# Attention scores from row-tiled products of q and k in place of stacked copies, and three heads of four transposed by DMA

## The reference: what is computed

```python
h = jnp.maximum(_layernorm(x, axis=-1), 0.0)
q = split_heads(h @ Wq.T); k = split_heads(h @ Wk.T); v = split_heads(h @ Wv.T)
bias = (adj + adj)[:, None]
a = jnp.einsum('bhnd,bhmd->bhnm', q, k) * D ** (-0.5) + bias
row_nonzero = jnp.any(a != 0, axis=-1, keepdims=True)
a = jnp.where(row_nonzero, a, -jnp.inf)
p = jax.nn.softmax(a, axis=-1)
p = jnp.where(jnp.isnan(p), 0.0, p)
o = jnp.einsum('bhnm,bhmd->bhnd', p, v)
x = x + merge_heads(o) @ Wo.T
```

## Time and profile before

| what | value |
|---|---|
| median of 3 runs | 1202.02 us (1201.95 to 1202.43) |
| the profiled execution, its own time | 1201.87 us |
| its span in the profile | 1200.1 us |
| PE (matmul) busy | 1131.5 us, 94% |
| PEld (weight load) busy | 803.0 us, 67% |
| DVE busy | 973.2 us, 81% |
| ACT busy | 973.3 us, 81% |
| POOL busy | 693.8 us, 58% |
| DMA queue q1 | 156.57 MB, 58.6% of 16 engines |

### The profile page before, as it was taken

One profiled execution on the slowest core, in us unless ns is written; L12 is line 12 of the kernel. 1 busy time (PEld: TensorE's weight loads), 2 busy tenths in 40 slices (PEclk: granted clock), 3 DMA queues, 4 the chain that ended last, 5 costly groups with the idle time before them and its releaser, 6 DMA issues.

```text
span 1200.1 us, 32321 instructions
## 1 busy us (share of the span) xinstructions
PE 1131.5 (94%) x10068; PEld 803.0 (67%) x10068; DVE 973.2 (81%) x3418; ACT 973.3 (81%) x3155; POOL 693.8 (58%) x939
## 2 busy tenths in 40 slices
PE   6789999999999999999999999999999999999997
PEld 5557766667766666766666776666776666776664
DVE  6888788888788888778888778888878887878884
ACT  3588888888888888888888888888888888888886
POOL 1346666656666656666655666655666655666655
PEclk9999999999999999999999999999999999999999
DMA  6345656565665665665565665655665565666654
GB/s 221 81 103 116 142 139 133 127 143 113 142 137 138 124 145 111 142 139 137 124 147 109 141 141 134 134 140 110 138 142 134 135 137 113 136 145 133 138 107 115
DMA packets 327193, 158.62 MB, mean 132 GB/s; under 512 B 279152, under 2 KB 287600, under 8 KB 327024
## 3 DMA queue, kind: packets, MB, share of 16 engines
q1 hardware_dynamic: 327024, 156.57, 58.6%
HBM read 47.45 MB, written 16.78 MB: 54 GB/s over the span
## 4 chain that ended last, share of the span: by engine, by line
PE 77%; DVE 17%; issue 4%; ACT 1%; DMA 1%; DVEq 0%; POOLq 0%; SPq 0%; POOL 0%; ACTq 0%
PE ps L998 44%; DVE k_stack L777 9%; PE ps L1014 9%; PE ps L1029 8%; DVE logits L727 6%; PE ps L1063 6%; PE ps L1068 5%; PE ps L878 2%; PE ps L1042 2%; DVE w_max L650 1%; ACT probs L527 1%; DMA w_nat<-in_L_gnn_Wq 1%; DVE x_res L804 0%; DVE row_min L727 0%; DVE w_lo L690 0%
## 5 line engine op out<-in xcount | busy, mean ns | idle before, releaser
L527 ACT ACTIVATE probs<-logits,row_min 128x256 f32<-128x256 f32 x1024 | 509.0, 502 | 67.1 <-DVE row_min L727 66.9
L727 DVE CUSTOM_DVE_ANT_0 logits<-ps,adj_s,sigma 128x256 f32<-128x256 f32 x1024 | 451.9, 479 | 52.5 <-PE ps L1014 50.4
L424 POOL TENSOR_TENSOR p<-probs,p 128x512 f16<-128x512 f32 x256 | 302.7, 1183 | 159.3 <-ACT p L540 158.6
L998 PE MATMUL ps<-ht_hi,w_hi 128*128 128x256 f16 x1024 | 280.4, 274 | 0.6 <-DVE q_lo L763 0.6
L998 PE MATMUL ps<-ht_hi,w_lo 128*128 128x256 f16 x1024 | 280.0, 273 | 0.0
L998 PE MATMUL ps<-ht_lo,w_hi 128*128 128x256 f16 x1024 | 279.8, 273 | 0.0
L1014 PE MATMUL ps<-k_stack,q_stack 96*128 96x256 f16 x1024 | 198.0, 275 | 38.7 <-DVE k_stack L777 38.7
L433 POOL TENSOR_TENSOR norm<-recip,some 128x256 f32<-128x256 f32 x128 | 85.7, 670 | 197.4 <-DVE some L744 197.3
L527 ACT ACTIVATION_READ_ACCUMULATOR probs<-logits,row_min 128x1 f32 x1024 | 198.5, 194 | 0.0
L1014 PEld LDWEIGHTS ps<-k_stack,q_stack 96*128 96x128 f16 x1024 | 82.8, 98 | 144.4 <-issue 63.0
L1029 PE MATMUL ps<-ident,probs 128*128 128x128 f32 x1024 | 154.1, 273 | 6.4 <-ACT probs_t L551 6.4
(11 more groups left out here) (86 smaller groups left out, 2065.9 us busy)
## 6 DMA issues: line engine op xcount, KB each, us to landing
xs<-in_x SPq DMA_DIRECT2D x34, 512.0 KB, 4.1
q_stack<-q_hi SPq DMA_DIRECT2D x256, 64.0 KB, 2.0
x_res<-in_x SPq DMA_DIRECT2D x32, 512.0 KB, 4.0
out<-x_res SPq DMA_DIRECT2D x64, 256.0 KB, 2.5
adj_raw<-in_adj SPq DMA_DIRECT2D x33, 256.0 KB, 4.8
q_stack<-q_lo SPq DMA_DIRECT2D x128, 64.0 KB, 2.0
pt<-p SPq DMA_TRANSPOSE x256, 3.1
w_nat<-in_L_gnn_Wq SPq DMA_DIRECT2D x1, 1024.0 KB, 6.0
```

Of the source, the lines that this page charges most:

```text
L424: g.tensor_tensor(p16[:, c % 2, k, 1], probs[:, h % 4].rearrange("p u n -> p (u n)"), p16[:, c % 2, k, 0], ALU.subtract).then_inc(p_split, 1)
L527: e = a.activation(probs[:, h % 4, u, :], logits[:, h % 4, u, :], ACT.Exp, bias=row_min[:, t.par(d), u, h:h + 1], scale=-1.0, accum_out=ro ...
L727: v.tensor_tensor_reduce(out=logits[:, h % 4, u, :], in0=ps[:, S_BANK + S_OF[h], N * u:N * u + N], in1=adj_s[:, t.par(d), u, :], scale=sig ...
L998: m = mm(o, l, r, start=start, stop=stop)
```

## The change

1. The stacks are gone. `scores` takes a whole group at once: for each half of the queries and each of the three products, the four heads in turn, each from the 32 partitions where its q and k lie. The four lie in four row tiles (32*128) of the array and write to four PSUM banks. It runs once every four steps, after the projection of steps 0, 4, 8 and 12, and waits until all eight logit units of the group before are done. q_hi, q_lo, k_hi and k_lo are doubled, by batch parity. The twelve DMAs to q_stack and the twelve copies to k_stack fall away.
2. `XJ = (0, 1, 2)`: three heads of four go by ScalarE rounding, GpSimd split and DMA transpose; only head 3 is transposed by TensorE. It goes to `AUX_BANK`, at the start of steps 0, 4, 8 and 12, and VectorE instead of ScalarE copies it out (`take_probs_t`). The bank of the transposed probabilities is freed. `AUX_USES` writes down the order in which the bank is used.
3. v is split when it leaves PSUM: ScalarE writes v_hi, and an fp32 copy of the columns of head 3 (v_y); VectorE writes v_lo (`take_v`) and frees the bank. GpSimd's `split_v` falls away.
4. Steps move: `values` comes ahead of the projection of its step, logits of a group come as 3, 3 and 2 units in the three steps after its scores, `turn_h` is at steps 5 and 9, layernorm at 3, adj_s at 7, the input of the residual at 4, the output DMAs at 12 and 14. Statistics, layernorm and loads of batches past the last one are left out. The maximum of Wo is found in the first slot instead of the second.

The core of the diff:

```diff
-XJ = (0, 2)
+XJ = (0, 1, 2)
 YJ = tuple(j for j in range(HC) if j not in XJ)
 NX, NY = len(XJ), len(YJ)
-S_OF = (0, 1, 2) * 5 + (1,)
...
+        q_hi = sb("q_hi", [P, 2, NC, N], F16)
+        q_lo = sb("q_lo", [P, 2, NC, N], F16)
+        k_hi = sb("k_hi", [P, 2, NC, N], F16)
...
-        q_stack = sb("q_stack", [NK * HD, 2, HC, NC, N], F16)
-        k_stack = sb("k_stack", [NK * HD, 2, HC, NC, N], F16)
-        v_sb = sb("v_sb", [P, 2, NU, D])
+        v_hi = sb("v_hi", [P, 2, NU, D], F16)
+        v_lo = sb("v_lo", [P, 2, NU, D], F16)
+        v_y = sb("v_y", [P, 2, NU, NC, NY, HD])
...
+        AUX_USES = [("h", 0, 0), ("h", 0, 1)]
+        for b in range(-1, NB + 1):
+            slot_uses = [(0, y_key(b, -1)), (4, ("y", b, 0)), (8, ("y", b, 1)), (12, ("y", b, 2)),
+                         (13, ("row", b + 1))]
+            slot_uses += [(9, ("h", b + 2, 0)), (12, ("h", b + 2, 1))] if b < 0 else \
+                         [(5, ("h", b + 2, 0)), (9, ("h", b + 2, 1))]
+            for at, key in sorted(slot_uses):
+                if 0 <= key[1] < NB and not (key[0] == "y" and NY == 0):
+                    AUX_USES.append(key)
...
-                    if s in (5, 6) and t.nxt:
-                        if s == 5:
-                            need(sp, scores_ready, H * t.batch(0))
-                        sp.wait_ge(pj_hi, 4 * t.batch(1) + 2)
-                        for j in range(HC):
-                            stack(t, q_stack, s - 5, q_hi, j, q_stacked)
-                    if s == 7 and t.nxt:
-                        for g in range(2):
-                            sp.wait_ge(pj_taken[g], pj_taken_at(t, g))
-                        for j in range(HC):
-                            stack(t, q_stack, 2, q_lo, j, q_stacked)
-                    if s in (14, 15) and t.prev:
...
-                        scale_adj(t)
+                    split_probs(t, s)
                     if s == 0 and t.prev:
                         spread_norm(t, -1, NC - 1)
                     if s % 4 == 0 and s >= 4 and t.cur:
                         spread_norm(t, 0, s // 4 - 1)
-                    split_probs(t, s)
-                    if s == 1 and t.cur:
-                        split_v(t)
-                    if s == 2 and t.nxt:
+                    if s == 3 and later(t, 2):
                         layernorm(t, 2)
+                    if s == 7 and t.nxt:
+                        scale_adj(t)
...
-                need(act, *turned_before(t, d, h))
+                b, c, j = t.batch(d), h // HC, h % HC
+                if j in XJ:
+                    need(act, p_split, NC * NX * b + by_dma(h) - NX + 1)
+                elif b + c > 0:
+                    act.wait_ge(aux_full, aux_after(*y_key(b, c - 1)))
...
-                a.activation(v_sb[:, t.par(d), u, :], ps[:, PJ_BANK + u, :], ACT.Copy, scale=DOWN)\
-                 .then_inc(pj_taken[u], 1)
+                a.activation(v_hi[:, t.par(d), u, :], ps[:, PJ_BANK + u, :], ACT.Copy, scale=DOWN)\
+                 .then_inc(v_hi_ready, 1)
+                for k, j in enumerate(YJ):
+                    a.activation(v_y[:, t.par(d), u, :, k, :],
+                                 ps[:, PJ_BANK + u, :].rearrange("p (c j d) -> p c j d", c=NC, j=HC)[:, :, j, :],
+                                 ACT.Copy, scale=DOWN).then_inc(v_hi_ready, 1)
...
-            def logit_rows(t, s):
-                d, h = head(t, s)
+            def logit_rows(t, c, first_unit, last_unit):
...
                     return
-                dve.wait_ge(scores_ready, H * t.batch(d) + (h + 1))
-                if h == 0:
-                    dve.wait_ge(adj_scaled, t.batch(d) + 1)
-                need(dve, probs_ready, H * t.batch(d) + (h - 3))
-                for u in range(NU):
-                    v.tensor_tensor_reduce(out=logits[:, h % 4, u, :], in0=ps[:, S_BANK + S_OF[h], N * u:N * u + N],
+                b = t.batch(d)
+                if first_unit == 0:
+                    dve.wait_ge(scores_ready, NC * b + (c + 1))
+                    if c == 0:
+                        dve.wait_ge(adj_scaled, b + 1)
+                for n in range(first_unit, last_unit):
+                    h, u = HC * c + n // NU, n % NU
+                    need(dve, probs_ready, H * b + (h - 3))
+                    v.tensor_tensor_reduce(out=logits[:, h % 4, u, :],
+                                           in0=ps[:, S_BANK + h % HC, N * u:N * u + N],
                                            in1=adj_s[:, t.par(d), u, :], scale=sigma[:, 0:1], scalar=3e38,
...
+            def take_v(t, d, u):
+                dve.wait_ge(v_hi_ready, (1 + NY) * (NU * t.batch(d) + u + 1))
+                v.scalar_tensor_tensor(out=v_lo[:, t.par(d), u, :], in0=ps[:, PJ_BANK + u, :], scalar=DOWN,
+                                       in1=v_hi[:, t.par(d), u, :], op0=ALU.mult, op1=ALU.subtract)\
+                 .then_inc(pj_taken[u], 1)
             def take_qk(t, j):
...
+            LOGITS = {1: (0, 3), 2: (3, 6), 3: (6, 8)}
             def slot(t):
                 for s in range(H):
-                    if t.prev and s in residual_steps(t):
-                        residual(t, residual_steps(t).index(s))
-                    logit_rows(t, s + 3)
...
+                    if t.prev and s in (10, 12):
+                        residual(t, (s - 10) // 2)
+                    if s == 1 and t.cur:
+                        take_v(t, 0, 1)
+                    if s == 15 and t.nxt:
+                        take_v(t, 1, 0)
+                    if s in (3, 5, 7, 9) and t.nxt:
+                        take_qk(t, (s - 3) // 2)
+                    if s % 4:
+                        logit_rows(t, (s + 3) // 4, *LOGITS[s % 4])
                     if s % 4 == 3 and t.cur:
                         invert(t, 0, s // 4)
...
-                            ln_statistics(t, 2, 1)
+                            for u in range(NU):
+                                ln_statistics(t, 2, u)
+                        if s == (5 if t.first else 2):
                             ln_mean_var(t, 2)
-                        if s in (3, 5, 7, 9):
-                            take_qk(t, (s - 3) // 2)
-                        if s in (9, 10, 11):
-                            stack_k(t, *((0, (0, 2)), (0, (1,)), (1, (0, 2)))[s - 9])
-                        if s in (11, 12, 13, 14):
-                            stack_k(t, *((1, (1,)), (2, (0, 2)), (2, (1,)), (3, (0, 2)))[s - 11])
-                        if s == 14:
-                            stack_k(t, 3, (1,))
-                        if s == (10 if t.first else 6):
-                            check_adj(t)
...
-                d, h = head(t, s)
+            def scores(t, c):
+                d, c = group(t, c)
...
+                if c == 0:
+                    for g in range(2):
+                        pe.wait_ge(pj_taken[g], (NJ // 2) * b + 2)
+                need(pe, logits_ready, NU * (H * b + HC * c))
+                Q, K = (q_hi, q_lo), (k_hi, k_lo)
                 for u in range(NU):
-                    m = mm(ps[:, S_BANK + S_OF[h], N * u:N * u + N], q_stack[:, t.par(d), j, c, P * u:P * u + P],
-                           k_stack[:, t.par(d), j, c, :], start=True, stop=True)
+                    for i, (x, y) in enumerate(THREE):
+                        for j in range(HC):
+                            m = mm(ps[:, S_BANK + j, N * u:N * u + N],
+                                   Q[x][HD * j:HD * j + HD, t.par(d), c, P * u:P * u + P],
+                                   K[y][HD * j:HD * j + HD, t.par(d), c, :], start=(i == 0), stop=(i == 2))
                 m.then_inc(scores_ready, 1)
...
                         o = ps[HD * j:HD * j + HD, PV_BANK, 0:N]
+                        h = HC * c + j
...
+                            m = mm(o, v_y[:, t.par(d), mh, c, YJ.index(j), :],
                                    probs_t[:, c % 2, YJ.index(j), mh, :], start=(mh == 0), stop=(mh == NU - 1))
                             continue
                         k = XJ.index(j)
                         for i, (a, b) in enumerate(THREE):
-                            m = mm(o, v16[:, t.par(d), a, k, mh, c, :],
+                            m = mm(o, (v_hi, v_lo)[a][:, t.par(d), mh, HD * h:HD * h + HD],
...
-                    if not t.first:
-                        scores(t, s + 4)
-                    elif s == H - 2:
-                        scores(t, H)
-                        scores(t, H + 1)
-                    elif s == H - 1:
-                        scores(t, H + 2)
-                        scores(t, H + 3)
+                    if NY and s == 0 and t.prev:
+                        turn_probs(t, -1, NC - 1)
+                    if NY and s % 4 == 0 and s >= 4 and t.cur:
+                        turn_probs(t, 0, s // 4 - 1)
+                    if s == 3 and t.prev:
+                        values(t, -1, NC - 1)
+                    if t.cur and s >= 4 and s % 4 == 3:
```

(14 more changed lines are left out.)

256 lines of the change are left out of this document (99 added, 157 removed).

## The result

The changed kernel takes 1217.92 us (median of 4 runs, 1217.49 to 1218.6); the kernel before took 1202.22 beside it. The ratio is 1.0125, interval 1.0106 to 1.0143: 1.3% slower, where 6.5% faster was forecast. The span grew from 1200.1 to 1215.7 us.

A forecast was written before the change was run, and what follows sets the result against it. TensorE was taken as the bound, its slot falling from 35.93 to 33.6 us: 31 slots give 72.2, plus 3.7 and 2.2 at the ends, 78.1 us off the 1200.1 span; predicted 1124 us, range 1085 to 1178.

The forecast's parts named there:

- whether the others cover: VectorE, ScalarE, GpSimd and DMA per slot: stay off the path; four steps of 2.1 us cover a 3.1 us DMA transpose.
- what would make the prediction wrong: Per group or slot: S above 1.3 or below 0.86 us, or named waits over 1 us per slot.
- The sum of TensorE's work: TensorE's slot: 29.0 us left after removals plus 4.4 for four score groups, 33.4; 33.6 with short waits.
- S: TensorE time for one group of scores, 24 products in row tiles; taken as 1.1 us.
- The lower bound: Score group, row tiles overlapping fully: six rounds, 0.65 us, plus 0.21 entering and leaving, 0.86; without waits 1087 us.
- the upper one: Score group with no overlap of row tiles: 24 x 0.109 + 0.21 = 2.83 us.
- `values` at nothing: `values` on TensorE, with 18 fp16 and two fp32 products, costs no more; at worst 0.3 us per call.
- The ends: First and last slots: 3.7 us gained from k_stack copies gone, 2.2 from ScalarE's lighter last slot.
- Wo's maximum moves and cancels: First slot: finding Wo's maximum, 2.3 us, moves there from the second slot, with no net cost.
- Rival 1: Lockstep slips, VectorE or ScalarE sets the pace: slot 35.0 us, about 1167 us; chance 0.15.
- Rival 2: TensorE bound by the instructions it takes: at 0.044 us each, slot 35.1, about 1171 us; chance 0.06.
- Rival 3: Row tiles do not overlap in the scores: slot 40.5 us, time 1339 us, slower; chance 0.07.

The follow-up runs named there:

- experiment 1: The changed kernel with `values` put back behind the projection of its step; 1112.76 us, ratio 0.9246.
- experiment 2: The changed kernel with the norm_t copy moved first in ScalarE's step, TensorE's order unchanged; 1094.82 us, ratio 0.9101.
- experiment 5: The changed kernel with norm_t on ScalarE between the high parts and the exps; 1113.18 us, ratio 0.9259.
- norm_first: The changed kernel with the norm_t copy moved first in ScalarE's step, the same run as experiment 2; 1094.82 us, ratio 0.9101.
- experiment 9: norm_first with the spreading of Wo's maximum in step 15 of the first slot instead of step 11; 1092.34 us, ratio 0.9077.
- values_behind: The changed kernel with `values` put back behind its projection, the same run as experiment 1; 1112.76 us, ratio 0.9246.
- norm_between: The changed kernel with norm_t between the high parts and the exps, the same run as experiment 5; 1113.18 us, ratio 0.9259.
- both_moves: The changed kernel with `values` behind its projection and norm_t first in ScalarE's step; 1099.26 us, ratio 0.9139.

## Why the prediction was wrong

**The step that failed** is in the paragraph on whether the others cover: "None of this is on the path as long as steps stay in order." For `values` I worked out one of the things that it waits for, the last DMA transpose, and found some four steps of cover. It waits also for `norm_taken`, and that producer was not worked out. The change took 1.32 us of scores and transposes and one half projection (1.31) out from between P and `values`, 2.63 in all. There `values` could start at P + 1.62 + 2.63 = P + 4.25 against P + 2.30, so only 1.95 was to spare; norm_t kept its place behind a copy that itself waits for P, and behind two exps. Costed the same way as the DMA, P + 1.62 against P + 2.30 would have stood there, since half a projection, the copies, exp and norm_t can all be read in the trace of before. The price was four waits, 4.0 us of a 36.45 us slot, 31 times; experiments 1, 2 and 5 leave one short one, none and one of them by three different edits, and the slots shorten by 3.3, 3.9 and 3.2. My own line on what would make the prediction wrong, named waits above 1 us per slot, is what the profile shows.

**The sum of TensorE's work** was right: 29.0 + 4S. Norm_first's gapless slot of 32.42 gives S = 0.86, while I took 1.1 from the row of full-width weight loads: mis-sized by 0.24 a group, 1.0 a slot. The time of norm_first, 1094.8 us, is near the 1087 that I had for this S without waits; the rest is mostly in the ends. The lower bound, carried over from column tiles with 0.21 for entering and leaving, was exact, and the upper one far off. Going into the row tiles and back costs 0.21 us in the trace. The Trainium skill (TensorEngine Tiling (Array Packing), Key Properties) says that a change of tiling mode drains TensorE; the 0.21 us agree with a cost there, but no run shows that a drain is its cause. The estimate of 1.06 from the Trainium skill's ratio of 3.07 (TensorE: Matmul & The Clock Gate, Measured speedup vs the span model) is not borne out at 256 columns, where every 24 products went in six rounds of four. `values` at nothing was right: in norm_first, from the end of one projection (574.34 + 0.11 = 574.45) to the next (575.55), it takes 1.10 as before.

**The other engines** came out as summed, per slot: VectorE 27.4 (27.6 forecast), ScalarE 28.6 (28.5), GpSimd 23.2 (26.3 at most), DMA 0.70 x 36.45 = 25.5 (27.9 at most). The copy of a transposed head on VectorE, unseen before, took 0.689 us (L720, 88.2 us for 128) where I had taken 0.685.

**The ends** were forecast to give 5.9 us and cost 6.8. "Wo's maximum moves and cancels" was wrong: the spread waits 4.11 us and not 2.3, at a place where the clock then falls to its lower level; experiment 9 gets 2.6 us of span back. The end after the last row test took 43.2 us at a granted clock of 0.84 against 40.0 at 1.00. The waits for norm_t do not explain it: with one short wait left per slot the end took 41.9 at 0.83 in values_behind and 38.5 at 0.96 in norm_between, and with none 41.3 at 0.91 in norm_first and 38.0 at 0.96 in both_moves. It goes with the granted clock. In the change TensorE was busy for 0.30 of the 3 us from 1179.70, and 0.50 was granted for the 12 us from 1182.70; the kernel before has 1.00 throughout. Why these stretches are longer in one kernel than in another is open.

**The rivals.** Rival 1, ScalarE or VectorE setting the pace through an in-order place, had the right engine and the wrong place and reason: I looked for it at the score banks and at step 12, where slack was a matter of load, while ScalarE was only 78% busy and late by its order. Its price, 1.4 us a slot, was a third of the real one. Rival 2 (TensorE bound by its instructions) fell: 370 products with 368 loads went in 32.42 us without a gap. Rival 3 (row tiles do not overlap) fell by S = 0.86. The slower outcome came through a mechanism that had no chance of its own in my list.

Of the two theories on the waits, norm_t is shown by experiments 1, 2 and 5. That the k_lo label was wrong is shown by 2 alone. What stays open is why transposes behind `values` take 0.05 us longer, and the clock at the end.

## What to carry to other kernels

When an instruction is moved ahead, or work between it and its producers is taken out, go through every semaphore it waits for, and for each write the producer's time as a sum from a common event in that engine's own order, against the consumer's sum. Here a 0.37 us copy at the end of a step, on an engine with 22% idle time, cost 10% of the time (1217.9 against 1094.8 us); moving it to the step's top took four lines. And when a label of a wait names an engine, test it: remove the other candidate's delay and see whether the labelled wait stays.

## What the runs showed of the hardware that I had not expected

- Products of 32 rows in four row tiles overlap fully: 24 of 256 columns in six rounds of 0.109 us, with 24 loads of 128 columns of weights in the same 0.65 us, 0.027 each, less than the 0.038 that I had taken as the floor for such loads. Doubling them cost 0.66 us per group.
- TensorE begins products of different row tiles out of program order: three products of one head in a row still ran as rounds of four heads.
- With 16 DMA transposes in a slot of 30.9 us the DMA share reads 1.07 and 196 GB/s, yet they land in 3.8 us instead of 3.1, and TensorE waits for them only 11.1 us in the whole run. So a share above 1 by packet times did not mean here that DMA was the bound.
- One wait of 4.11 us in the first slot was followed by TensorE's 1.2 GHz level through the next projections and scores. In the steady slots waits of 0.6 to 1.6 us, four in 36.45 us, left the granted clock at 1.00.
- Four fp32 transposes take 0.49 us, start to next start, directly behind products in column tiles, and 0.44 behind a projection.
